# Graph convolution on one core: a fifth source chunk per turn by register-addressed column copies instead of an indirect gather

## The reference, cut to what matters

```python
h = relu(layernorm(x))
filters = silu(edge_attr @ fW1 + fb1) @ fW2 + fb2        # 206250 x 128
messages = (h[src] @ dW + db) * filters                  # one row of h per edge, by source
aggregated = segment_sum(messages, dst, num_segments=n)
x = x + (silu(aggregated @ uW1 + ub1) @ uW2 + ub2)
```

## Time and profile before

| | |
|---|---|
| median of 3 runs | 5505.33 us (5501.94 to 5513.48) |
| the profiled execution, its own time | 5491.89 us |
| its span, first to last instruction | 5490.1 us |
| busy: PE, VectorE (DVE), ScalarE (ACT), POOL | 3661.5, 3149.1, 2573.3, 2913.4 us |
| mean granted clock of TensorE | 0.566 |

### The profile page before, as it was taken

One profiled execution on the slowest core, in us unless ns is written; L12 is line 12 of the kernel. 1 busy time (PEld: TensorE's weight loads), 2 busy tenths in 40 slices (PEclk: granted clock), 3 DMA queues, 4 the chain that ended last, 5 costly groups with the idle time before them and its releaser, 6 DMA issues. The chain is left out here.

```text
span 5490.1 us, 88496 instructions
## 1 busy us (share of the span) xinstructions
PE 3661.5 (67%) x14349; PEld 2797.4 (51%) x14350; DVE 3149.1 (57%) x13756; ACT 2573.3 (47%) x14407; POOL 2913.4 (53%) x3066
## 2 busy tenths in 40 slices
PE   4666666566565666665656777767777767777777
PEld 2444444444444444444445556555555555565556
DVE  5666666666565666666644555555555554555554
ACT  4333434343343334433414555555555555555554
POOL 5555555555555555555545555545555555555553
PEclk6555555555555555555556556666566666656666
DMA  4112122121111112122132122121221211212211
GB/s 102 45 45 47 45 46 48 46 47 45 45 45 45 45 45 47 45 46 46 45 95 56 52 55 56 51 54 51 54 55 52 55 53 53 55 51 55 56 52 45
DMA packets 192455, 284.64 MB, mean 52 GB/s; under 512 B 84692, under 2 KB 137403, under 8 KB 187704
## 3 DMA queue, kind: packets, MB, share of 16 engines
q0 software_dynamic: 97088, 202.29, 15.3%
q1 hardware_dynamic: 90408, 40.70, 2.9%
q10 hardware_dynamic: 4840, 40.55, 2.4%
HBM read 264.60 MB, written 15.70 MB: 51 GB/s over the span
## 5 line engine op out<-in xcount | busy, mean ns | idle before, releaser
L63 POOL DMA_INDIRECT ae_xg<-table,ae_idx x1592 | 1506.0, 946 | 1188.1 <-issue 488.6
L63 POOL DMA_INDIRECT ce_xg<-table,ce_idx x1442 | 1368.2, 949 | 1282.7 <-DVE ce_msg L1797 806.6
L1634 ACT COPY ce_held<-sums 128x4 uint8 x11008 | 1232.6, 190 | 1013.2 <-issue 1003.5
L1761 DVE COPY ce_held<-sums 128x4 uint8 x8256 | 752.2, 184 | 631.5 <-issue 629.1
L1700 PE MATMUL ce_ps_h<-ce_ea,ce_fw 50*128 50x384 f32 x1076 | 661.6, 757 | 570.3 <-ACT ce_hid L1618 421.4
L1158 PE MATMUL ae_ps_k<-ae_xg,ae_e 128*96 128x129 f32 x3224 | 888.9, 433 | 6.9 <-remote 6.8
L1158 PEld LDWEIGHTS ae_ps_k<-ae_xg,ae_e 128*96 128x96 f32 x3224 | 685.8, 276 | 146.6 <-issue 120.6
L1669 PE MATMUL ce_ring<-ce_fw,ce_hid 128*128 128x128 f32 x3228 | 702.5, 402 | 1.9 <-issue 1.7
L1669 PEld LDWEIGHTS ce_ring<-ce_fw,ce_hid 128*128 128x128 f32 x3228 | 661.9, 309 | 60.6 <-issue 59.4
L1700 PEld LDWEIGHTS ce_ps_h<-ce_ea,ce_fw 50*128 50x128 f32 x1076 | 265.4, 272 | 732.9 <-ACT ce_hid L1618 360.1
L1678 PEld LDWEIGHTS ce_ring<-ce_hot,ce_msg 128*128 128x128 f32 x3224 | 537.0, 255 | 35.9 <-issue 35.8
(11 more groups left out here) (193 smaller groups left out, 4094.5 us busy)
## 6 DMA issues: line engine op xcount, KB each, us to landing
ce_stage<-table SPq DMA_DIRECT2D x2688, 0.5 KB
ae_stage<-table SPq DMA_DIRECT2D x2560, 0.5 KB
ce_ea<-in_edge_attr ACTq DMA_DIRECT2D x88, 450.0 KB
ae_xg<-table,ae_idx POOLq DMA_INDIRECT x1592
ce_xg<-table,ce_idx POOLq DMA_INDIRECT x1442
sums<-in_x SPq DMA_DIRECT2D x7, 448.0 KB, 4.8
sums<-features SPq DMA_DIRECT2D x1, 3136.0 KB
table<-sums SPq DMA_DIRECT2D x6, 462.0 KB, 3.8
```

Source lines behind the costliest of these rows:

```text
L63: eng.indirect_dma_start(out=out, out_offset=None, in_=table[:, :], in_offset=bass.IndirectOffsetOnAxis(ap=idx, axis=0)).then_inc(done, 16)
L1634: one = nc.scalar.copy(held_bytes[:, 4 * (m * P + k):4 * (m * P + k) + 4], by_byte[:, bass.ds(start, 4)])
L1761: one = nc.vector.tensor_copy(held_bytes[:, 4 * (m * P + k):4 * (m * P + k) + 4], by_byte[:, bass.ds(start, 4)])
```

## The change

It makes the table `COLUMNS` five entries: four whole chunks (for the slots 0, 1, 2 and 3) and 64 columns of the chunk of slot 4, 576 columns a turn. VectorE copies 304 of them, 48 or 56 a slot in place of 32; ScalarE 272, 48 or 40 a slot as before, but 48 in the slots 2 and 5. POOL gathers 31 chunks a turn in place of 32. The row of offsets for VectorE is split into two halves like that for ScalarE, so that SP issues four small transfers ahead of the loop in place of three. The two loop heads move to other places of their blocks. The attribute loads stay on ScalarE.

```diff
--- before.py
+++ after.py
@@ -539,7 +539,7 @@
     body(0, True, SL)
     for i in range(1, OPEN + 1):
         body(i, False, SL)
-    with nc.Fori(OPEN + 1, SHUT, engines=[engine], hint_back_edge=True, head_slot={engine: 140}) as i:
+    with nc.Fori(OPEN + 1, SHUT, engines=[engine], hint_back_edge=True, head_slot={engine: 128}) as i:
         body(i, False, SL)
     body(SHUT, False, REST)
 
@@ -570,7 +570,7 @@
 
 
 CARRY_SLOT = 4
-COLUMNS = (Column(0, 3, False, 55, 73), Column(2, 5, False, 55, 73), Column(3, 1, True, 55, 73), Column(CARRY_SLOT, 2, True, 27, 37))
+COLUMNS = (Column(0, 3, False, 67, 61), Column(1, 4, False, 67, 61), Column(2, 5, False, 66, 62), Column(3, 1, True, 70, 58), Column(CARRY_SLOT, 2, True, 34, 30))
 COLUMN_TURNS = TURNS - 2
 TO = [column.to for column in COLUMNS]
 ROWS = 64
@@ -597,8 +597,8 @@
         return self.held[self.start(s):self.start(s + 1)]
 
 
-SCALAR = Share([48, 40, 40] * 2, [range(c.vector, c.count) for c in COLUMNS])
-VECTOR = Share([2 * READ] * SL, [range(c.vector) for c in COLUMNS])
+SCALAR = Share([48, 40, 48] * 2, [range(c.vector, c.count) for c in COLUMNS])
+VECTOR = Share([48, 56, 48] * 2, [range(c.vector) for c in COLUMNS])
 
 
 def collects(i):
@@ -667,7 +667,7 @@
 
     body(0, True, SL)
     body(1, False, SL)
-    with nc.Fori(2, TURNS - 1, engines=[engine], hint_back_edge=True, head_slot={engine: 160}) as i:
+    with nc.Fori(2, TURNS - 1, engines=[engine], hint_back_edge=True, head_slot={engine: 25}) as i:
         body(i, False, SL)
     body(TURNS - 1, False, REST)
 
@@ -1536,9 +1536,10 @@
         (w_in, steps, key_ready, begun, cleared, s_hid, s_act, s_flt, s_bias, s_msg, s_sum, s_acc) = (
             sem("c_" + k) for k in "w_in steps key_ready begun cleared hid act flt bias msg sum acc".split())
         drawn = sb("drawn", [COLUMN_TURNS, SCALAR.total + VECTOR.total], i32)
-        columns = sb("columns", [65, COLUMN_TURNS * VECTOR.total], i32)
-        half = SCALAR.start(SL // 2)
-        by_row = [drawn[:, 0:half], drawn[:, half:SCALAR.total], drawn[:, SCALAR.total:]]
+        by_half = [list(zip((share.start(0), share.start(LOAD)), (share.start(LOAD), share.total))) for share in (SCALAR, VECTOR)]
+        columns = sb("columns", [97, COLUMN_TURNS * max(b - a for ends in by_half for a, b in ends)], i32)
+        in_half = [ends[0][1] for ends in by_half]
+        assert all(b - a == width for ends, width in zip(by_half, in_half) for a, b in ends)
         held = sb("held", [P, len(COLUMNS), P])
         held_bytes = held[:, :, :].rearrange("p m e -> p (m e)").bitcast(u8)
         by_node, by_byte = planes[:, 2, 0:NP], planes[:, :, :].rearrange("p t n -> p (t n)").bitcast(u8)
@@ -1560,8 +1561,10 @@
             sp.dma_start(drawn[:, :], a["column_rows"][:, :]).then_inc(lists_in, 16)
 
             sp.wait_ge(scaled, 2)
-            for k, width in enumerate((half, SCALAR.total - half, VECTOR.total)):
-                sp.dma_start(columns[32 * k:32 * k + 1, 0:COLUMN_TURNS * width].rearrange("o (t c) -> o t c", c=width), by_row[k]).then_inc(table_in, 16)
+            for k, (ends, first) in enumerate(zip(by_half, (0, SCALAR.total))):
+                for v, (a0, a1) in enumerate(ends):
+                    sp.dma_start(columns[64 * k + 32 * v:64 * k + 32 * v + 1, 0:COLUMN_TURNS * (a1 - a0)].rearrange("o (t c) -> o t c", c=a1 - a0),
+                                 drawn[:, first + a0:first + a1]).then_inc(table_in, 16)
 
             def tables(r):
 
@@ -1623,10 +1626,10 @@
                 def collect(i, s):
 
                     if s == 0:
-                        act.wait_ge(table_in, 16 * (r + 4))
+                        act.wait_ge(table_in, 16 * (r + 5))
                         act.sem_inc(begun, 1)
                     starts = sources_at(nc, mybir.EngineType.Activation, columns[32 * (s // LOAD):32 * (s // LOAD) + 1, :],
-                                        (i - 1) * half + SCALAR.start(s) % half, SCALAR.counts[s])
+                                        (i - 1) * in_half[0] + SCALAR.start(s) % in_half[0], SCALAR.counts[s])
                     for (m, k), start in zip(SCALAR.slot(s), starts):
                         if k == SCALAR.first[m]:
                             act.wait_ge(s_column, column_at(r, i, m) + 1)
@@ -1750,10 +1753,11 @@
                     if not collects(i):
                         return
                     if s == 0 and not piece:
-                        dve.wait_ge(table_in, 16 * (r + 4))
+                        dve.wait_ge(table_in, 16 * (r + 5))
                         dve.sem_inc(begun, 1)
-                    part = VECTOR.slot(s)[piece * READ:(piece + 1) * READ]
-                    starts = sources_at(nc, mybir.EngineType.DVE, columns[64:65, :], (i - 1) * VECTOR.total + VECTOR.start(s) + piece * READ, len(part))
+                    part = VECTOR.slot(s)[READ:] if piece else VECTOR.slot(s)[:READ]
+                    starts = sources_at(nc, mybir.EngineType.DVE, columns[64 + 32 * (s // LOAD):65 + 32 * (s // LOAD), :],
+                                        (i - 1) * in_half[1] + VECTOR.start(s) % in_half[1] + piece * READ, len(part))
                     for (m, k), start in zip(part, starts):
                         if k == VECTOR.first[m]:
                             dve.wait_ge(s_column, column_at(r, i, m) + 1)
```

## The result

The changed kernel takes 5602.7 us (median of four runs, 5576.5 to 5607.1) beside 5509.4 us of the kernel before: a ratio of 1.0163, 95% interval 1.0129 to 1.0197. It is slower, as forecast, and by a third of what was forecast: some 93 us where the prediction had 297. The profiled execution took 5600.8 us, its span is 5599.0 us.

The account below looks back on a forecast made before the run. ScalarE was taken to bound the kernel before, VectorE the changed one: 5491.9 us (profiled execution) + 297 (43 turns x 6.9 us) + 0.6 (SP) = 5790 us, range 5530 to 5890 us.

Parts of the forecast that it names:

- VectorE becomes the bound: First case, convolution turn: VectorE needs 66 us against 59.1, adding 297 us; own range 5730 to 5865 us, chance 0.62.
- the price of the stall: VectorE's copies in the convolution: each costs 0.077 us of "issue" besides 0.091 us busy, also for 304 copies a turn.
- faster, by parted gathers: Rival: later messages part runs of ten gathers, saving ScalarE 2.8 us a turn, net 1.3; 5436 us, chance 0.09.
- lower bound of 64.9 us: VectorE's turn from below: 64.9 us, the stall thinned out as gathers fill a smaller part of a longer turn.
- ScalarE stays the bound: Rival: VectorE's slack hides its added copies; ScalarE adds 1.0 to 2.4 us a turn, 5535 to 5595 us, chance 0.16.
- One gather less: On POOL: one gather fewer a turn gives ScalarE back 0.8 us of crawl; POOL's own time was already covered.
- Copies in the way of the message: VectorE: 80 of 112 added copies stand between bias-add and multiplication, so each slot's `ce_msg` is later; no separate size.
- ScalarE waits several us a turn: Sign of the first case: ScalarE, which almost never waited, would wait several us a turn for PE.
- Gathers not stretched: Added VectorE copies do not lengthen POOL's gathers: 1399 gathers of still 0.95 us.
- Loop heads, PE, SP: VectorE's longer loop at nothing (else 82 us), PE's extra product hidden (else 30 us), SP's extra transfer 0.6 us once.
- No change: Rival: removed gather and added copies cancel on ScalarE, VectorE hidden; 5492 us, chance 0.05.
- heavier: Rival: VectorE's 112 added copies hold up gathers by 10.2 us a turn; turn 70 us, 5961 us, chance 0.08.

Follow-up runs that it names:

- experiment 1: The change with copies split 288/288, then 336/240 (VectorE/ScalarE), in place of 304/272: 5533.8 us and 5687.8 us.
- experiment 4: The change with POOL waiting for the next slot's message before every other slot, so two slots' gathers come together: 5940.2 us, ratio 1.0789.
- 6 with one fill and two: The kernel before with one or two dependent fills of a spare tile on GpSimd behind each slot's gathers: 5352.3 us and 5223.1 us.
- experiment 2: The kernel before with one gather a turn less and nothing in its place: 5417.4 us; the change with a 32nd gather put back: 5661.5 us.
- experiments 5 and 6: 5: kernel before with 224 copies on each engine, 5449.1 us; 6: register loads or fills on POOL, in that or the kernel before, 5162.9 to 5546.0 us.
- 224/224 version: The kernel before with 32 copies a turn moved from ScalarE to VectorE, 224 on each: 5449.1 us, ratio 0.9894.

## Why the prediction was wrong in size

**VectorE becomes the bound: right.** Its waits for PE vanished, and the chain runs through its copies. Its busy time, by the two stretches of 3100 to 5300 us (us, then busy of PE, PEld, DVE, ACT, POOL), before:

```profile
3100.00:5300.00 2200.00, 1626.43 (x6701) 1273.07 (x6702) 1164.95 (x8252) 1251.80 (x9781) 1126.85 (x1189) 0.62 0.20 54
```

and after:

```profile
3100.00:5300.00 2200.00, 1663.67 (x6491) 1340.33 (x6491) 1501.28 (x11945) 1269.66 (x9930) 1047.41 (x1105) 0.57 0.19 50
```

1164.95 / 2200 x 59.3 = 31.4 us a turn have become 1501.28 / 2200 x 61.8 = 42.2: 10.8 more, where the added copies and the `place` were put at 10.2 + 0.3.

**The step that failed is the price of the stall**, "the same price for 304" copies, thinned out to the lower bound. 66 us less 42.2 us busy charges 23.8 us of loss a turn; it was 19.1 and some 0.5 that no releaser has. Two things were wrong in it. The 0.077 us of "issue" was multiplied by the number of copies, and experiment 1 shows that it does not grow with them: it would have been right to add one lump. (With the 25.0 us that ScalarE bore as the bound the sum would have been much the same; the two ways to reckon differ for other numbers of copies.) And that lump was held to follow the gathers' share of the turn, when it follows how they are cut into runs (experiment 4, and 6 with one fill and two, where ScalarE is the bound). Between VectorE's points of 3.0 and 6.0 runs, the 5.1 runs of the kernel before would give it 21.3 us; so of the 4.7 us charged too much, about 2.2 are the runs and 2.5 the price per copy. That is a line through two points and no measurement: the change with just 5.1 runs a turn was not tried.

**The rival "faster, by parted gathers" named the mechanism**, on ScalarE and with 2.8 us a turn. It came about on the engine that had become the bound, whose messages now come evenly. I had set it against "VectorE becomes the bound", as another case; it was part of it. The price was within reach: the earlier trace rows show that a run's first 26 copies are fast.

**The lower bound of 64.9 us was no bound.** It let the stall shrink only with the gathers' share. The time lies in the wide range all the same, by luck: near the rival "ScalarE stays the bound" (5535 to 5595), whose mechanism did not come about, since VectorE waits for nobody, and outside the first case's own range from 5730.

**One gather less: right in kind**, 0.8 to 1.8 us a turn where 0.8 was put (experiment 2). **Copies in the way of the message:** all 112 added ones stand between the bias-add and the multiplication, 16 in four slots and 24 in two, and not 80; no term of the sum rests on that count.

**ScalarE waits several us a turn: by its waits that name PE or "remote", only (19.3 + 14.4 + 8.2) / 38.8 = 1.1 us**, 8.2 us of them ahead of `one_hid`; its "issue" ahead of the Silu rose from 68.5 us to 152.3, in stretches of up to 7.7 us, which the profile does not name; whether they are waits for PE stays open.

**Gathers not stretched: right.** 948 ns, with 304 copies a turn as with 192. The rule of the Trainium skill, SBUF — State Buffer, section "SBUF: two separate sides", that VectorE can hold GpSimd out of the port pair they share, did not bite through these copies.

**Loop heads, PE, SP, at nothing or 0.6 us:** no wait of VectorE for any of them shows. What a loop head costs could stand in "issue", whose longest stretch is 1.6 us, beside 1.9 before. SyncE is no bound in the change either, where it waits (290.7 + 200.7) / 30.7 = 16.0 us a turn in 3100 to 5000 us; in experiments 5 and 6 it makes POOL late or bounds the turn itself.

**No change** and **heavier** are excluded by the interval and the gathers' length.

## What to carry to other kernels

When an engine stands in "issue" beside another engine's work, don't price that wait per instruction: find what it goes with (here a run of indirect gathers) and charge it once per occurrence to whichever engine is the bound. A change that moves the bound also changes who meters the others, so ask again how they will bunch. And where short instructions crawl during a burst, try cutting the burst: three tiny dependent fills behind each slot's gathers were worth 5.4% here, more than any share of the copies; POOL had the time, until SyncE or POOL itself filled the turn. Then look for the next engine in the same crawl: SyncE, with its small transfers, has 0% of the chain in both kernels and heads it once the others are quicker.

## What the runs showed of the hardware

- While a run of indirect gathers is on, ScalarE and VectorE issue about one short instruction in 0.7 to 1.4 us. SyncE does too: in the kernel before with three fills its single-row transfers begin 1.4 to 2.1 us apart between 4034.93 and 4039.89 us, late in a run of six gathers that began at 4031.45, and 0.3 us apart in the 2 us behind it. The crawl does not go with the bytes: 9.73 MB or 78.98 MB in 2400 us, at 32 packets a gather, cost 22.5 and 19.1 us a turn. What holds them up (the sequencers, the packets' writing) no run tells; it stays open.
- It sets in only some 4 us into a run, and a break of 1.3 to 2.3 us on POOL is enough to begin anew. The longer break does more: 22.2, 20.9 and 19.4 us of "issue" a turn on ScalarE for one fill, two and three, the last with SyncE as the bound.
- A long fill on GpSimd holds up VectorE's copies. In the 224/224 version with one fill of 128 x 3072, VectorE's copies by line over 3100 to 5000 us:

```profile
L1770 DVE COPY ce_held<-sums 128x4 uint8 x6943 | 861.1, 372 | 263.8 <-issue 254.9 <-PE ce_ring L1694 4.0
```

  and one of them in its timeline, beside a fill that began at 4026.01 and took 2.68 us:

```profile
4026.62 2.10 DVE L1770 COPY ce_held<-sums 128x4 uint8 x1 [1.17 <-issue]
```

  372 ns on average and 2.10 us for this copy of 4 bytes a partition, which ends with the fill; without fills the mean is 184 ns. The Trainium skill, SBUF — State Buffer, section "SBUF: two separate sides", says that the shared port pair is an exclusive lock for a whole instruction, whoever starts first; here the trace agrees, with GpSimd as the holder. In the stretch none of VectorE's copies ends inside one of the 186 fills, over 0.1 us from either end, and 615 of ScalarE's do. Beside fills of 0.31 us the mean is 193 to 203 ns.
- Instructions of POOL's sequencer alone make no break between gathers: they are done while earlier gathers run.
